# One common task order in each attention step becomes five, one for each engine, and a small tile moves

## The chip, the cores and the metric

One NeuronCore of one Trainium2 chip. The metric is the device time of one execution in microseconds, from the core's first to its last instruction with what lies around them. It has five engines with queues of their own: TensorE (PE), VectorE (DVE), ScalarE (ACT), GpSimd (POOL) and SyncE (SP), which here only issues DMAs.

## What is computed

Sixteen batches of 256 rows of 512 numbers (x) and of 256 rows of 384 (ctx) go through four residual blocks:

```python
x = x + _L0_xattn_ref(_layernorm(x), ctx_768, ctx_768, ...)   # q, k normed over the row; 16 heads of 32; + Qp, layer norm
x = x + _L0_ffn_ref(_layernorm(x), L0_ffn_weight)             # Hadamard turn, 4-bit rounding, ternary weight
x = x + _L1_xattn_ref(_layernorm(x), ctx_768, ...)            # 16 heads of 32, scores clipped at 1e4
x = x + _L1_ffn_ref(_layernorm(x), W1, b1, W2, b2)            # ternary 512 -> 2048, gelu, ternary 2048 -> 512
```

## The kernel before, in words

Products are made in float16 halves: a float32 operand is split into an upper half (a cast, on ACT) and a lower half (the rest, on DVE or POOL), and three products of halves stand for one. PSUM has 8 banks of 128x512 float32, and every product that is later read holds one.

The first three blocks run as a pipeline of four parts. Step i of 19 works on batch i in part "0f" (layer norm, query, key and value of attention 0), on batch i-1 in "0b" (the 16 heads of attention 0, its output, and the whole of the first feed-forward block), on batch i-2 in "1f" (the same front for attention 1, and the maxima of its scores), and on batch i-3 in "1b" (the heads of attention 1 and its output). Steps 3 to 15 have all four parts; I call them the steady steps. The last block is phase B, which comes behind the 19 steps and works on pairs of batches.

Each part is a list of tasks (`front_0`, `heads_of`, `back`, `front_1`). A task is a small piece that several engines share. What the lines of the profile are:

- `load` (SP, L657, L658, L663): fetches x and ctx of the next batch. For x it waits until the turned keys of the batch before have left the tile. `fetch` (SP, L643, L645, L650): the residual rows of a block; L650 is that of attention 1 and is needed by DVE at `out 1,0`.
- `stats` (DVE L1072, L1074, then POOL L783 to L789): mean and 1/deviation. `normalise` (ACT L887). `turn_x` (PE L1341 transposes, ACT L892 upper half, DVE L1083 lower half). `split_ctx` (ACT L910, DVE L1116).
- `project 0,k,j,late` (PE L1321 to L1325, each 128x512, 6 matmuls or 3): half of one projection. `bias` (ACT L917 squares or L925 upper half of a value, DVE L1126 or L1131). `unit` (ACT L932, DVE L1142). `unit_turn` (SP L688, DMA transposes).
- `project_turned` (PE L1331 to L1335), `split_qk` (ACT L943, DVE L1150).
- `scores` and `maxima` (PE L1473, 24 matmuls of 32 rows for four heads); `clip` (DVE L1169, attention 1 alone, in PSUM); `shift` (PE L1400, four matmuls that need all four clips); `reduce` (DVE L1157).
- `head l,n`: ACT takes exp of head n (L955) and the upper half of head n-1 (L963); POOL the lower half of head n-1 (L816); PE attends with head n-4 (L1495 to L1497, 12 matmuls of 33 or 32 columns, which wait for POOL's lower half); DVE divides four heads at a time (L1254). The exponentials lie in a ring of 5 slots (`pf`), the halves in rings of 4 (`ph`, `pl`): ACT's upper half of head h waits until PE has attended with head h-4.
- `out_project`, `out` (DVE L1185, L1188), `post_norm`, `turn_ffn`, `hadamard` (PE L1433), `absmax`, `round`, `levels`, `turn_levels` (SP L692), `ffn0` (PE L1443), `ffn0_out` (DVE L1223, POOL L828).
- In the last three steps `signs n` (DVE L1065 and L1067) makes the ternary weights of phase B, and `stats_b`, `norm_b` (L1077), `split_b` (L1089) and SP's transposes L611 its first input. PE's first matmuls of phase B are L1508.

The order is a string of digits: each takes the next task of that part's list. Every engine emits its instructions in this one order, skipping tasks in which it has nothing. The choice of banks (`banks_of`) is made from the same order. So an engine cannot be ahead of another in the order, only in time; it waits by semaphores.

```python
def task_order(i):
    ...
    order = ORDERS[i] if i in ORDERS else [n for n in ORDER if active[int(n)]]
    return [(PART[task], task) for task in merged(streams, order)]
...
def steps(emit):
    ...
        tasks = task_order(i)
        uses, counts = plan([task for _, task in tasks], base)
        emit(tasks, i, i % 2, {**kept, **uses})
```

## Time and profile before

| | us |
|---|---|
| median of 3 runs (lowest, highest) | 1842.26 (1839.59, 1843.07) |
| the profiled execution's own time | 1841.57 |
| its span, first to last instruction | 1839.7 |
| PE busy | 1651.1 (90%) |
| DVE busy | 1243.9 (68%) |
| ACT busy | 1017.6 (55%) |
| POOL busy | 987.0 (54%) |
| mean granted TensorE clock | 0.955 of full |

A share of busy time is a mean over stages. Matmuls are pipelined and their ends are modelled, so a stretch in which PE is "busy" can hold more or less work; PE's idle time and who ended it, and the chain of work followed back from the end, say more. The granted clock is 1.00 at 2.4 GHz and 0.50 at 1.2 GHz; in a row over a longer stretch it is the mean.

### The profile page before, as it was taken

What the parts mean: (1) busy time and instruction counts of PE and PEld (TensorE: products, weight loads), DVE (VectorE), ACT (ScalarE), POOL (GpSimd) and SP (SyncE); (2) the same over time, 40 slices, a digit from 0 to 9 for tenths busy, and PEclk for the clock granted to TensorE, in tenths of its full rate; (3) what the DMA queues carried; (4) which work ended last, traced back from release to release, by engine and by line L of the source; (5) the groups of instructions that cost most, each with busy time, mean ns of one, the idle gap of its engine ahead of it and who ended that gap; (6) DMA issues with size and microseconds to landing.
All of it is one profiled execution on the core that took longest, in us unless ns stands there. A gap on an engine that the chain in (4) does not pass through costs nothing.

```text
span 1839.7 us, 43874 instructions
## 1 busy us (share of the span) xinstructions
PE 1651.1 (90%) x17746; PEld 952.3 (52%) x17746; DVE 1243.9 (68%) x2428; ACT 1017.6 (55%) x1873; POOL 987.0 (54%) x1073
## 2 busy tenths in 40 slices
PE   5688999999999999989999999987748999999999
PEld 2445656556565555655556565564423444444444
DVE  4758778797887978779788787858873444343432
ACT  4663867658686585866758677586342222222221
POOL 2653857658585585856758576582461323322231
PEclk9889999999999999999999999978859999999999
DMA  7132231312304133131431313246222221221210
GB/s 249 53 112 58 68 113 25 113 40 87 113 14 114 30 107 97 29 113 28 110 93 34 113 28 111 63 138 195 92 73 54 69 69 32 60 61 54 69 47 23
DMA packets 168215, 144.80 MB, mean 79 GB/s; under 512 B 125256, under 2 KB 131528, under 8 KB 166992
## 3 DMA queue, kind: packets, MB, share of 16 engines
q1 hardware_dynamic: 165712, 133.62, 25.9%
q0 software_dynamic: 2304, 8.39, 1.1%
q8 instruction: 142, 2.33, 0.5%
q14 instruction: 57, 0.47, 0.1%
HBM read 72.77 MB, written 31.46 MB: 57 GB/s over the span
## 4 chain that ended last, share of the span: by engine, by line
PE 50%; DVE 27%; DMA 7%; issue 6%; ACT 5%; POOL 4%; SPq 1%; DVEq 1%; ACTq 0%; POOLq 0%
PE psum L1518 10%; PE psum L1508 9%; DVE psum L1169 6%; PE psum L1321 5%; PE psum L1322 5%; PE psum L1325 5%; DVE arena L1157 4%; PE psum L1473 4%; PE psum L1433 3%; PE psum L1341 2%; DMA arena<-in_x 2%; DVE arena L1072 2%; DVE arena L1198 2%; DMA out<-arena 2%; PE psum L1495 2%
## 5 line engine op out<-in xcount | busy, mean ns | idle before, releaser
L816 POOL TENSOR_TENSOR arena<-arena 128x512 f16<-128x512 f32 x512 | 597.8, 1190 | 125.9 <-ACT arena L963 125.9
L955 ACT ACTIVATE arena<-psum 128x512 f32<-128x512 f32 x512 | 304.9, 603 | 81.1 <-PE psum L1400 63.6
L963 ACT ACTIVATE arena<-arena 128x512 f16<-128x512 f32 x512 | 323.8, 640 | 16.5 <-PE psum L1497 16.5
L1321 PE MATMUL psum<-arena 128*128 128x512 f16 x672 | 263.9, 393 | 21.6 <-DVE arena L1083 15.1
L1006 ACT ACTIVATE arena<-psum,arena 128x512 f32<-128x512 f32 x128 | 88.0, 687 | 338.5 <-PE psum L1508 338.5
L1322 PE MATMUL psum<-arena 128*128 128x512 f16 x672 | 262.2, 390 | 0.0
L1325 PE MATMUL psum<-arena 128*128 128x512 f16 x672 | 261.6, 389 | 0.0
L848 POOL TENSOR_TENSOR arena<-arena 128x512 f16<-128x512 f32 x64 | 79.8, 1247 | 326.1 <-DVE arena L1276 326.1
L1508 PE MATMUL psum<-arena 128*128 128x512 f16 x1024 | 243.7, 381 | 8.0 <-DMA arena<-arena 8.0
L1518 PE MATMUL psum<-arena 128*128 128x512 f16 x1016 | 240.1, 379 | 3.3 <-POOL arena L848 3.2
L1495 PE MATMUL psum<-arena 128*128 128x33 f16 x2048 | 192.7, 180 | 44.8 <-POOL arena L816 43.4
L1276 DVE CAST arena<-arena 128x512 f16<-128x512 f32 x128 | 55.4, 433 | 253.0 <-ACT arena L1006 253.0
L1495 PEld LDWEIGHTS psum<-arena 128*128 128x128 f16 x2048 | 166.5, 97 | 90.5 <-issue 40.6
L828 POOL TENSOR_TENSOR arena<-arena 128x512 f32<-128x512 f32 x32 | 40.4, 1268 | 289.3 <-DVE arena L1223 288.5
L1473 PE MATMUL psum<-arena 32*128 32x256 f16 x4608 | 165.7, 276 | 29.7 <-ACT arena L955 7.9
L1497 PE MATMUL psum<-arena 128*128 128x33 f16 x2048 | 189.9, 178 | 0.0
L1496 PE MATMUL psum<-arena 128*128 128x32 f16 x2048 | 189.9, 178 | 0.0
L1169 DVE TENSOR_SCALAR psum<-psum 128x512 f32<-128x512 f32 x256 | 160.6, 690 | 42.6 <-PE psum L1473 42.5
L1496 PEld LDWEIGHTS psum<-arena 128*128 128x128 f16 x2048 | 164.3, 97 | 16.2 <-issue 1.0
L1508 PEld LDWEIGHTS psum<-arena 128*128 128x128 f16 x1024 | 100.6, 98 | 130.6 <-issue 11.2
L1518 PEld LDWEIGHTS psum<-arena 128*128 128x128 f16 x1016 | 98.8, 98 | 125.0 <-POOL arena L848 6.7
L1497 PEld LDWEIGHTS psum<-arena 128*128 128x128 f16 x2048 | 162.7, 97 | 0.0
(125 smaller groups left out, 3085.7 us busy)
## 6 DMA issues: line engine op xcount, KB each, us to landing
arena<-in_x SPq DMA_DIRECT2D x32, 512.0 KB, 4.3
arena<-x_scratch SPq DMA_DIRECT2D x32, 512.0 KB, 3.9
arena<-in_L_ffn_W SPq DMA_DIRECT2D x16, 1024.0 KB, 5.4
arena<-arena SPq DMA_DIRECT2D x16, 512.0 KB, 6.2
x_scratch<-arena POOLq DMA_DIRECT2D x16, 512.0 KB, 5.6
x_scratch<-arena SPq DMA_DIRECT2D x16, 512.0 KB, 3.0
out<-arena SPq DMA_DIRECT2D x14, 512.0 KB, 4.2
arena<-in_ctx SPq DMA_DIRECT2D x16, 384.0 KB, 5.3
```

The source lines that it names most:

```text
L816: gp.tensor_tensor(pl[l][:, h % NP, :], pf[l][:, h % NF, :], ph[l][:, h % NP, :], ALU.subtract).then_inc(p_lo[l].sem, 1)
L955: sc.activation(pf[l][:, h % NF, :], bank(u.bank), ACT.Exp, scale=SCALE / (QS * QS) if l == 0 else SCALE).then_inc(read[u.bank], 1)
L963: sc.activation(ph[l][:, h % NP, :], pf[l][:, h % NF, :], ACT.Copy).then_inc(p_hi[l].sem, 1)
L1169: v.tensor_scalar(bank(u.bank), bank(u.bank), CLAMP / SCALE, -CLAMP / SCALE, ALU.min, ALU.max).then_inc(clipped.sem, 1)
L1321: te.matmul(out, x_hi, w[:, 0, c, :], start=(c == 0), stop=False)
L1322: te.matmul(out, x_hi, w[:, 1, c, :], start=False, stop=False)
L1325: mm = te.matmul(out, x_lo, w[:, 0, c, :], start=False, stop=(c == chunks - 1))
L1495: te.matmul(out, p_hi_t, vs[l][:, k, h, 0:OW], start=(k == 0), stop=False)
L1496: te.matmul(out[:, 0:HD], p_hi_t, vs[l][:, k, h, HD + 2:VP], start=False, stop=False)
L1497: mm = te.matmul(out, p_lo_t, vs[l][:, k, h, 0:OW], start=False, stop=(k == NT - 1))
L1508: mm = te.matmul(bank(4 + f % 2), w1T[:, c, f * P:(f + 1) * P], xTb[slot][:, part, c, :], start=(c + part == 0), stop=(c + part == DC))
L1518: mm = te.matmul(bank(k), src[:, f % NG, k * P:(k + 1) * P], w2T[:, f, :], start=(f + n == 0), stop=(f + n == FC))
```

## The change

`task_order` and `steps` take an engine, and the tables hold one string for each of SP, POOL, ACT, DVE and PE in each step (one set, "steady", for steps 3 to 15). Banks and semaphore counts follow PE's order. Every task and every instruction is kept; only their order on each engine differs. The tile `row_of` (the rows that choose a bias) shrinks from 8 words to 2 and moves from the front of SBUF to a place just ahead of `vs`. All tiles between start 8 words lower; `vs`, `levels0` and the rings `pf` and `ph` start 6 words lower, so at 8 bytes past a multiple of 64 where they were at 32. Two targets of DMA transposes in the rings (`nT` and `xTb`) begin 6 words further in and so keep their addresses.

```diff
-ORDER = ("2001111112202000110100120110101030111011033113331200330301313312003311031123031121332233310133333313"
...
 ORDERS = {
...
+    "steady": {
+        "SP": ("2010000000000000000011111111111111111111111111111111111111111111111111100000000031333333333333333333"
...
+ENGINES = ("SP", "POOL", "ACT", "DVE", "PE")
...
-def task_order(i):
+def task_order(i, engine):
...
-    order = ORDERS[i] if i in ORDERS else [n for n in ORDER if active[int(n)]]
+    order = ORDERS.get(i, ORDERS["steady"])[engine]
...
-def steps(emit):
+def steps(emit, engine):
...
-        tasks = task_order(i)
-        uses, counts = plan([task for _, task in tasks], base)
-        emit(tasks, i, i % 2, {**kept, **uses})
+        uses, counts = plan([task for _, task in task_order(i, "PE")], base)
+        emit(task_order(i, engine), i, i % 2, {**kept, **uses})
...
-        row_of = take(8)[:, 0:2].bitcast(F16)
...
+        row_of = take(2).bitcast(F16)
...
-        nT = ph_raw[0][:, NT * D // 2:NT * D].bitcast(F16).rearrange("p (c n) -> p c n", c=DC)
+        nT = ph_raw[0][:, NT * D // 2 + 6:NT * D + 6].bitcast(F16).rearrange("p (c n) -> p c n", c=DC)
...
-        xTb = [pf_raw[0][:, 0:DC * BT * P].bitcast(F16).rearrange("p (s c n) -> p s c n", s=2, c=DC)]
+        xTb = [pf_raw[0][:, 6:DC * BT * P + 6].bitcast(F16).rearrange("p (s c n) -> p s c n", s=2, c=DC)]
```

In the changed kernel every line of the engines' bodies stands 68 lower (L955 is L1023 there).

First place: PE in a steady step, around the `shift` of the first four heads of attention 1. Before, behind the attention matmuls of head 12:

```order
L1497 MATMUL psum<-arena 128x33
L1400 MATMUL psum<-arena 128x512 x4
L1321 MATMUL psum<-arena 128x512
L1322 MATMUL psum<-arena 128x512
L1325 MATMUL psum<-arena 128x512
```

Now, behind those of head 13:

```order
L1565 MATMUL psum<-arena 128x33
L1389 MATMUL psum<-arena 128x512
L1390 MATMUL psum<-arena 128x512
L1393 MATMUL psum<-arena 128x512
L1389 MATMUL psum<-arena 128x512
L1390 MATMUL psum<-arena 128x512
L1393 MATMUL psum<-arena 128x512
L1468 MATMUL psum<-arena 128x512 x4
L1563 MATMUL psum<-arena 128x33
```

The shift has moved behind one more head (13) and behind half a projection. Also, the two halves of `project 0,1,0`, which stood on either side of the attention of head 5 (task `head 0,9`), now stand on either side of that of head 9 (task `head 0,13`).

Second place: ACT in a steady step, the two squares of the query (L917, now L985) among the heads of attention 0. Before:

```order
L963 ACTIVATE arena<-arena 128x512
L917 ACTIVATE arena<-arena 128x512
L955 ACTIVATE arena<-psum 128x512
L963 ACTIVATE arena<-arena 128x512
L955 ACTIVATE arena<-psum 128x512
L963 ACTIVATE arena<-arena 128x512
L917 ACTIVATE arena<-arena 128x512
L955 ACTIVATE arena<-psum 128x512
```

Now:

```order
L1031 ACTIVATE arena<-arena 128x512
L985 ACTIVATE arena<-arena 128x512
L1023 ACTIVATE arena<-psum 128x512
L1031 ACTIVATE arena<-arena 128x512
L985 ACTIVATE arena<-arena 128x512
L1023 ACTIVATE arena<-psum 128x512
```

The first square stood behind `head 0,9` and the second behind `head 0,11`; now they stand behind `head 0,13` and `head 0,14`, so the heads 9 to 12 no longer queue behind them.

Third place: DVE in the last of the 19 steps, around its last two `signs`. Before:

```order
L1067 SCALAR_TENSOR_TENSOR arena<-arena 128x2048
L1169 TENSOR_SCALAR psum<-psum 128x512 x4
L1251 RECIPROCAL arena<-psum 128x8
L1254 TENSOR_TENSOR arena<-psum,arena 128x128 x2
L1169 TENSOR_SCALAR psum<-psum 128x512 x4
L1251 RECIPROCAL arena<-psum 128x8
L1254 TENSOR_TENSOR arena<-psum,arena 128x128 x2
L1065 TENSOR_SCALAR arena<-arena 128x2048
L1067 SCALAR_TENSOR_TENSOR arena<-arena 128x2048
L1072 BN_STATS arena<-arena 128x6
```

Now:

```order
L1135 SCALAR_TENSOR_TENSOR arena<-arena 128x2048
L1237 TENSOR_SCALAR psum<-psum 128x512 x4
L1319 RECIPROCAL arena<-psum 128x8
L1322 TENSOR_TENSOR arena<-psum,arena 128x128 x2
L1133 TENSOR_SCALAR arena<-arena 128x2048
L1135 SCALAR_TENSOR_TENSOR arena<-arena 128x2048
L1237 TENSOR_SCALAR psum<-psum 128x512 x4
L1319 RECIPROCAL arena<-psum 128x8
```

The last `signs` has moved ahead of the last four clips.

SP in a steady step: `fetch 1` (the residual rows of attention 1, L650, now L718) stood ahead of the transposes, right behind the context's store. Now:

```order
L763 DMA ctx_scratch<-arena 128x768
L756 DMA_TRANSPOSE arena<-arena 128x8x128 x2
L760 DMA_TRANSPOSE arena<-arena 128x4x128
L756 DMA_TRANSPOSE arena<-arena 128x8x128 x2
L718 DMA arena<-x_scratch 128x1024
L760 DMA_TRANSPOSE arena<-arena 128x4x128
```

It now stands behind both `unit_turn`s and the first `turn_levels`, each of which waits for DVE.

## Rows read from the trace of the kernel before

**Rows 1.** Busy time by stretch: span, PE, PEld, DVE, ACT, POOL, granted clock, DMA, GB/s.

```profile
290.00:367.90 77.90, 72.89 (x978) 45.50 (x977) 61.78 (x127) 54.44 (x106) 51.73 (x59) 0.98 0.26 75
...
1068.40:1146.20 77.80, 72.77 (x979) 45.61 (x978) 61.60 (x128) 54.63 (x106) 51.63 (x59) 0.98 0.26 75
...
1300.00:1380.00 80.00, 47.69 (x641) 29.27 (x638) 61.82 (x96) 28.59 (x55) 39.71 (x28) 0.73 0.23 73
```

**Rows 2.** Chain of waits, 600 to 760: start, us, what (x's load in two steps).

```profile
643.90 5.12 DMA arena<-in_x
...
721.79 5.12 DMA arena<-in_x
```

**Rows 3.** Chain of waits, 640 to 680, around that load.

```profile
642.29 0.70 DVE arena L1185
...
654.77 1.84 DVE arena L1116
...
657.27 0.39 PE psum L1321
```

**Rows 4.** Busy time by stretch, as rows 1: heads of attention 0, and after.

```profile
648.30:671.00 22.70, 19.46 (x329) 13.79 (x328) 12.29 (x27) 22.12 (x44) 19.48 (x21) 0.99 0.36 130
664.50:670.60 6.10, 4.46 (x132) 3.39 (x127) 4.46 (x13) 5.82 (x13) 5.24 (x6) 0.99 0.01 3
670.60:674.00 3.40, 3.40 (x13) 1.24 (x10) 3.25 (x7) 3.40 (x7) 3.37 (x4) 0.52 0.02 5
```

**Rows 5.** Who PE waited for, 664.5 to 671: total us, times, longest.

```profile
PE psum L1495 <- POOL arena L816: 1.1, 2, 0.7
```

**Rows 6.** ACT in order of time: start, us, line, operation, [idle before <-releaser].

```profile
662.12 0.62 ACT L917 ACTIVATE arena<-arena 128x512 bf16<-128x512 f32 x1
...
664.78 0.63 ACT L963 ACTIVATE arena<-arena 128x512 f16<-128x512 f32 x1 [0.45 <-PE psum L1497]
```

**Rows 7.** POOL in order of time, lower halves of three heads.

```profile
669.99 3.38 POOL L816 TENSOR_TENSOR arena<-arena 128x512 f16<-128x512 f32 x3
```

**Rows 8.** Chain of waits, 640 to 680: one matmul at either clock, four scores.

```profile
657.66 0.22 PE psum L1322
...
659.03 0.77 PE psum L1473 x24
...
671.22 0.43 PE psum L1322
```

**Rows 9.** DVE in order of time: `unit` beside an idle POOL, then a busy one.

```profile
628.33 1.47 DVE L1142 SCALAR_TENSOR_TENSOR arena<-arena 128x512 f16<-128x512 f32 x2
...
672.34 2.25 DVE L1142 SCALAR_TENSOR_TENSOR arena<-arena 128x512 f16<-128x512 f32 x2
```

**Rows 10.** DVE in order of time: a residual add, `out 1,0`.

```profile
640.31 0.69 DVE L1185 SCALAR_TENSOR_TENSOR arena<-psum,arena 128x512 f32<-128x512 f32 x1
```

**Rows 11.** DMAs that touch the scratch tensors, whole program.

```profile
DMA to landing us min/median/max: 2.7/3.9/7.7
```

**Rows 12.** DVE in order of time, last step.

```profile
1355.77 2.49 DVE L1169 TENSOR_SCALAR psum<-psum 128x512 f32<-128x512 f32 x4 [4.49 <-PE psum L1473]
...
1358.81 1.28 DVE L1065 TENSOR_SCALAR arena<-arena 128x2048 f16<-128x2048 f32 x1
1360.12 3.34 DVE L1067 SCALAR_TENSOR_TENSOR arena<-arena 128x2048 f16<-128x2048 f32 x1
```

**Rows 13.** Chain of waits, 1340 to 1400.

```profile
1360.15 7.66 POOL arena L816 x5
...
1379.88 0.61 DVE arena L1089
...
1386.60 3.59 PE psum L1508 x8
```

**Rows 14.** ACT in order of time: a write into the values' tile, one elsewhere.

```profile
645.97 0.60 ACT L925 ACTIVATE arena<-psum 128x512 f16<-128x512 f32 x1 [6.97 <-PE psum L1325]
...
651.74 0.61 ACT L943 ACTIVATE arena<-psum 128x512 f16<-128x512 f32 x1
```

103 lines of the change are left out of this document (84 added, 19 removed).

## The prediction

> **What bounds the kernel now.** I read the busy time by stretch first. From 290 to 1146 us it shows 11 equal stretches of which the first and the last stand in [rows 1]; PE is busy some 73 of 77.8 us in each and DVE 62. So PE is the bound, with little slack, and whatever the change saves in a step it saves 13 times. The chain of waits gives the step's length, as the distance of two equal events: 721.79 - 643.90 = 77.89 us [rows 2]. The third row of [rows 1] is part of the drain, the last steps before phase B, where PE is busy 47.7 of 80 us at a mean clock of 0.73: most idle time for each step lies there.
>
> PE's idle time in a steady step is one thing and its wasted time another. I cut the step along the chain into pieces:
>
> Piece A, the load. The residual add `out 1,1` ends (642.29 + 0.70), only then does SP issue x's load, which lands 5.12 us after 643.90; statistics, normalising, transposes and `split_ctx` follow, and PE's first projection starts at 657.27 [rows 2, 3]. The chain is 14.3 us long, and PE fills most of it with other work.
>
> Piece B, the heads of attention 0, 648.3 to 671.0. ACT is busy 22.1 of 22.7 us and PE only 19.5 [rows 4]: here ACT, not PE, is full. In its last part PE waits 1.1 us for POOL's halves [rows 5], and ACT once waits 0.45 for PE to release a ring slot [rows 6]. So the ring goes round through all three.
>
> Piece C, right behind. From 670.60 the granted clock is 0.52, that is the 1.2 GHz level, for 3.4 us; in the 6.1 us before, at 2.4 GHz, PE was busy 4.5 us, all of it attention matmuls of 33 columns and 32-row scores [rows 4]. In 9 of the 11 stretches the mean is 0.98 as in [rows 1], in two it is 1.00: the fall comes in most steps. It hits projections: 0.43 us a matmul where 0.22 is usual [rows 8]. Eight of them lose 1.7 us.
>
> The Trainium skill ("TensorE: Matmul & The Clock Gate", Part 1) says that idleness throttles the array and sustained activity releases it. By that alone this fall would not be there, since no wait of PE near it is over 0.7 us, and the change could not take it away. The trace disagrees: the clock falls behind a stretch that is 73% busy.
>
> **The change part by part, steady steps.** All counts are per step.
>
> 1. ACT's two squares go behind heads 13 and 14 instead of 9 and 11. Each costs 0.62 us [rows 6], so heads 10 and 11 come 0.6 us sooner on ACT and head 12 1.2 us sooner, and PE's attention, which has 2 halves of a projection less ahead of it, releases the slots before ACT asks (the 0.45 goes). What is late next is POOL: 3.38 / 3 = 1.13 us a head [rows 7], which cannot start before 652.4, when it has made the deviations. 14 heads end at 652.4 + 14 x 1.13 = 668.2. I walk PE beside that: the projection starts at about 658.3 (ACT now does one more head before the context's split, but it starts 0.5 sooner; DVE does `split_qk 1,1,1`, 0.6 us, ahead of the first `split_x`), so 1.0 later than 657.27, but with one more head and a `scores` task done, 1.2 us of work (0.77 and the wait at its start [rows 8]; a head is 12 matmuls 25 ns apart, 0.3). PE then finds every head ready until head 13 and starts the next projection at 668.8; before, it started at 670.6, a head (0.3) less and a shift (0.4) more done. Gain 1.8 + 0.3 - 0.4 = 1.7 us.
> 2. The clock. The narrow stretch shrinks from 6.1 us to the 2.6 us between the second half of `project 0,1,0` and the next projection. I expect the fall to go there. It is worth 1.7 us on PE.
> 3. DVE takes this back in part. `stats 1` (1.7 us) is out of its way, but behind the scores of 667.1 it has four clips, the guard, a division, `unit` (2.25 beside a busy POOL [rows 9]), a division, two clips, a bias and two clips: the second shift can go at 676.8 to 677.1, before at 679.2. So of 1.7 + 1.7 = 3.4 us, 2.1 to 2.4 are kept. DVE is late next.
> 4. `split_out` and `turn_x 1,1`: PE waits some 0.3 us more for DVE there. Kept: 1.8 to 2.0.
> 5. `unit 0,1` moves ahead of `split_ffn 0,1`, from beside an idle POOL (1.47 us for two) to beside a busy one (2.25) [rows 9]. It delays the second Hadamard by 0.2 us; what follows waits for the values' biases, which come when they did. The `unit` itself is off the path. Cost 0 to 0.2. If one sorts by the Trainium skill instead ("SBUF — State Buffer", Who interferes with whom: a DVE instruction with two SBUF inputs and a GpSimd one that reads SBUF exclude each other), each of the two would stand a whole POOL subtraction; the row shows 0.4 more for each, so I keep the row.
> 6. The tail of the step: `shifts 1,1` moves ahead of the last bias and of `ffn0_out`, and the next step's scores start 0.5 us sooner; but `out 1,1` has one more `reduce` before it, and the load chain starts 0.2 later. As piece A is set by the load, not by PE, the 0.5 buys nothing and the 0.2 is paid.
> 7. SP's `fetch 1` is issued behind the transposes, at about 633.5. It lands 3.9 us later [rows 11], so at 637.4 to 638, and is wanted at about 639 (640.31 before [rows 10], the queue ahead of it shorter). Cost 0 now; the cover is one microsecond.
>
> Sum for a steady step: -1.8 us, times 13: **-23.4 us**.
>
> **The last step.** DVE idles 4.49 us before its last clips, and behind them spends 1.28 + 3.34 on the last `signs` [rows 12]. Now the `signs` fill the idle time. POOL's last five halves, on the chain, took 7.66 us beside them [rows 13], 5 x 1.13 = 5.65 without: 2.0 us. Then `norm_b` and `split_b` no longer queue behind the residual adds: the last `split_b` ended at 1380.5 and gated the transposes and PE's first matmul at 1386.60 [rows 13]; it needs four norms (0.5), two output splits (0.7), four splits (0.6 to 1.2) behind the last division, about 8.3 us from 1366.7 instead of 11.6 from 1368.9. **-5.5 us**.
>
> **The other five ragged steps** (0, 1, 2, 16, 17). Every order differs. No row prices that. From below: an order made for each engine could cost as much as it saves, +3. From above: PE waits about 70 us there, most for chains through DVE that no order shortens; a quarter is 17. I take **-4**, nearer the low end since the tasks at the longest waits (the `turn_ffn` of step 1, the shifts of step 17) keep their places.
>
> **The tile.** The rings now start 8 bytes past a multiple of 64. The nearest rows are ACT's cast into the values' tile, whose rows lie 132 bytes apart, 0.60 us, and the same cast into an even tile, 0.61 [rows 14]. So 0. A price is kept among the rivals.
>
> Sum: -23.4 - 5.5 - 4 = -33 us on the profiled execution's own 1841.6 us; its median is 0.7 higher. **Forecast 1809 us.**
>
> **The rivals.**
> - The clock falls all the same, in piece C or before the first projection, where heads 0 to 3, two transposes and a `scores` now stand together, 5 us of narrow work. For it: that stretch is nearly as long as today's. Against: a wide `project_turned` stands right ahead of it, and today's front, 4 us long, brings no fall. Half a projection before the shift and half behind it, at half clock, put the next scores 1.9 us later, of which DVE hides 0.7: 1.2 us a step. 13 x 0.6 + 9.5 = 17: **1825 us**.
> - The gain does not go round. Piece A runs from DVE's `out 1,1` to the load and is not shortened by the change. If PE's denser pieces only make it wait longer for the load (DVE, 62 of 78 us, leaves the end of the step no room), only the last step's 5.5 stays: **1836 us**.
> - Slower: the late residual. DVE's `out 1,0` stands in line ahead of `out 1,1`, and that issues x's load. If `fetch 1` lands later than 1 us behind my reckoning, each step is longer by the rest. The landing times go up to 7.7 us [rows 11]: then 7.7 - 3.9 - 1.0 = 2.8 us x 13 = 36, **1845 us**. It decides from a landing of 7.4 us on. Against: 3.9 is the median, and six small transposes are its only company.
> - The rings' place costs. Every head's work on POOL, ACT and PE touches them. In piece B POOL is late next, so 0.3 us on each subtraction is 16 x 0.3 = 4.8 us a step, x 13 = 62: **1871 us**. It decides from 0.16 us on each (1.13 to 1.29).
> - The orders could hold only in name, if a semaphore made an engine wait for what the common order implied. None is added, and the waits name the task that they need. Under 1 in 100.
>
> **How the numbers follow.** A measurement of this kernel can tell a change from no change from about 0.2% (3.7 us) on. Forecast 0.55, clock 0.2, no round 0.11, late residual 0.08, rings 0.06. The range goes down to 1797, for up to 12 us more from the ragged steps or 0.9 more a step, and up to 1836, so that the two slower rivals and half of the tail of the third are left out. Faster: 0.55 + 0.2 + 0.11 less a part that ends within 3.7 us, 0.84; within 0.2%: 0.06; slower: 0.10.
>
> **What would show it.** The distance of two x loads is 76.1 us. The granted clock reads 1.00 in most stretches of a step. PE's wait for POOL in piece B is under 0.6 us. POOL's subtraction stays 1.13 us from start to start. `out 1,0` waits for PE and not for a DMA. In the last step DVE's `signs` lie before the last clips and phase B's first matmul starts 5 to 6 us earlier, counted from the last `shift`. Wrong if the step stays over 77.3, if the last of PE's waits is for DVE's L1237, or if the clock still reads 0.98.

## The result, and the profile after

The changed kernel takes **1827.84 us** (median of 4 runs, 1825.35 to 1830.4) against 1842.66 for the kernel before (4 runs beside them): ratio 0.9923, 95% interval 0.9904 to 0.9943. It is faster, by 14.8 us where 33 were forecast. Its profiled execution took 1826.25 us, with a span of 1823.8 (1839.7 before).

Every line of the changed kernel stands 68 lower than before: POOL's subtraction L816 is L884, the shift L1400 is L1468, `unit` L1142 is L1210, the residual add L1185 is L1253.

Busy time by stretch of the kernel after. The first row is one step from load to load, beside [rows 1]; the next two are the two longest steps; the last two are a piece of attention 0's heads and what follows it, beside [rows 4].

```profile
800.73:877.04 76.31, 72.08 (x981) 45.29 (x979) 62.70 (x128) 54.56 (x105) 50.71 (x58) 1.00 0.28 76
500.40:578.40 78.00, 73.59 (x986) 45.69 (x982) 62.62 (x127) 54.86 (x107) 50.87 (x59) 0.98 0.24 69
578.40:658.40 80.00, 73.88 (x997) 46.62 (x994) 62.59 (x127) 54.82 (x107) 52.21 (x60) 0.98 0.27 79
...
821.40:827.50 6.10, 5.96 (x110) 3.49 (x109) 4.01 (x11) 5.82 (x14) 5.61 (x7) 1.00 0.01 3
827.50:830.90 3.40, 3.32 (x56) 1.95 (x53) 3.37 (x7) 3.40 (x8) 3.16 (x6) 1.00 0.63 43
```

The piece in which PE was 73% busy is now 98% busy, and the clock behind it reads 1.00 in place of 0.52. The chain of waits, x's load in two steps, and below it the same for the longest step:

```profile
800.73 5.04 DMA arena<-in_x
...
807.94 0.21 POOL arena L852
808.21 0.73 POOL arena L853
809.20 4.92 POOL arena L884 x4
...
877.04 5.55 DMA arena<-in_x
```

```profile
569.36 4.09 DMA arena<-in_x
...
644.52 7.40 DMA arena<-in_x
```

This step is 877.04 - 800.73 = 76.31 us against 77.89 in [rows 2]; the ten steps without a fall of the clock (I call them quiet) take 75.16 to 77.51, 76.55 in the mean. Most of that spread is the load's: from its landing to PE's first shift there are 21.2 us in each quiet step, and so there were before. Two steps are not quiet: in that from 500.4 the clock fell, and in that from 578.4 it fell and the load took 7.40 us to land.

The page's groups of POOL's subtraction and of its add, before and after (total us, mean ns):

```profile
L816 POOL TENSOR_TENSOR arena<-arena 128x512 f16<-128x512 f32 x512 | 597.8, 1190 | 125.9 <-ACT arena L963 125.9
...
L828 POOL TENSOR_TENSOR arena<-arena 128x512 f32<-128x512 f32 x32 | 40.4, 1268 | 289.3 <-DVE arena L1223 288.5
```

```profile
L884 POOL TENSOR_TENSOR arena<-arena 128x512 f16<-128x512 f32 x512 | 579.8, 1160 | 116.6 <-ACT arena L1031 114.8
...
L896 POOL TENSOR_TENSOR arena<-arena 128x512 f32<-128x512 f32 x32 | 34.4, 1094 | 302.1 <-DVE arena L1291 302.1
```

The same two instructions are shorter, and I had forecast that they would not be. In order of time POOL did 13 subtractions in 14.48 us, 1.11 each where [rows 7] had 1.13 by the same division; one of the 13 took 1.80, and those that nothing disturbs start 1.05 apart, for 1.11 to 1.12 before:

```profile
809.16 14.48 POOL L884 TENSOR_TENSOR arena<-arena 128x512 f16<-128x512 f32 x13
```

PE's waits in that step, and DVE around the two Hadamard products of attention 0 in it:

```profile
PE psum L1563 <- POOL arena L884: 2.2, 4, 1.1
PE psum L1501 <- DVE arena L1151: 0.6, 1, 0.6
```

```profile
853.91 0.68 DVE L1151 TENSOR_TENSOR arena<-psum,arena 128x512 f16<-128x512 f32 x1
854.51 3.16 DVE L1210 SCALAR_TENSOR_TENSOR arena<-arena 128x512 f16<-128x512 f32 x2
857.59 0.68 DVE L1151 TENSOR_TENSOR arena<-psum,arena 128x512 f16<-128x512 f32 x1
```

`unit 0,1` (L1210) stands between the two splits (L1151) that the products wait for, and took 3.16 us where I had priced 2.25 [rows 9]. Taken one by one, beside POOL, the two of [rows 9] and, below them, the two here:

```profile
672.22 1.15 POOL L816 TENSOR_TENSOR arena<-arena 128x512 f16<-128x512 f32 x1
...
672.34 1.58 DVE L1142 SCALAR_TENSOR_TENSOR arena<-arena 128x512 f16<-128x512 f32 x1
...
673.84 0.74 DVE L1142 SCALAR_TENSOR_TENSOR arena<-arena 128x512 f16<-128x512 f32 x1
```

```profile
854.51 1.66 DVE L1210 SCALAR_TENSOR_TENSOR arena<-arena 128x512 f16<-128x512 f32 x1
854.53 1.09 POOL L884 TENSOR_TENSOR arena<-arena 128x512 f16<-128x512 f32 x1 [1.22 <-ACT arena L1031]
...
855.58 1.54 POOL L884 TENSOR_TENSOR arena<-arena 128x512 f16<-128x512 f32 x1
...
856.09 1.57 DVE L1210 SCALAR_TENSOR_TENSOR arena<-arena 128x512 f16<-128x512 f32 x1
```

So 2.25 was no price for two beside a busy POOL: the first met a subtraction and took 1.58, the second met none and took 0.74. The first ended 0.55 us after the subtraction that it met (672.22 + 1.15 = 673.37, 672.34 + 1.58 = 673.92), and so did both of the later two (0.55 after 855.62 and 0.54 after 857.12). The subtraction that starts beside a waiting `unit` is longer too, 1.54 for 1.09.

The last step, chain of waits, beside [rows 12, 13]:

```profile
1350.63 0.61 PE psum L1468 x4
...
1363.56 3.34 DVE arena L1157 x2
...
1369.59 3.17 DMA arena<-arena
...
1372.90 1.90 PE psum L1576 x8
```

From the last shift to phase B's first matmul there are 1372.90 - 1350.63 = 22.3 us; before, 1386.60 - 1358.32 = 28.3 with the matmul of [rows 13] and this row for the shift:

```profile
1358.32 0.61 PE psum L1400 x3
```

**Where the time went.** I cut both traces at `split_ctx` of step 3 and of step 15 and at phase B's first matmul. Steps 0 to 2: 187.7 us before, 192.7 after, **+5.0**. Twelve steady steps: 933.0 and 925.2, **-7.8**. The drain from there: 265.9 and 254.9, **-11.0**. Phase B, whose order is untouched: 453.1 and 450.9, -2.2. Together -15.9, the difference of the spans.

### The profile page after: what moved, and what is told of

Read it like the earlier page. It is cut to its first block, busy times and chain, and to the rows that moved or that the text cites. A ratio compares the mean times of both kernels' runs of the same rounds, so it can differ in the third digit from the quotient of the medians.

```text
span 1823.8 us, 43897 instructions
## 1 busy us (share of the span) xinstructions
PE 1638.3 (90%) x17746; PEld 945.1 (52%) x17746; DVE 1242.2 (68%) x2428; ACT 1015.8 (56%) x1873; POOL 959.1 (53%) x1073
## 4 chain that ended last, share of the span: by engine, by line
PE 46%; DVE 31%; POOL 8%; DMA 6%; issue 4%; ACT 2%; SPq 2%; DVEq 1%; ACTq 0%; POOLq 0%
PE psum L1586 11%; PE psum L1576 11%; DVE psum L1237 8%; POOL arena L884 6%; PE psum L1389 4%; PE psum L1393 4%; PE psum L1390 4%; DMA arena<-in_x 4%; PE psum L1541 3%; DVE arena L1225 3%; DVE arena L1140 3%; DVE arena L1210 3%; DVE arena L1322 2%; DVE arena L1266 2%; DVE arena L1151 2%
## 5 line engine op out<-in xcount | busy, mean ns | idle before, releaser
L884 POOL TENSOR_TENSOR arena<-arena 128x512 f16<-128x512 f32 x512 | 579.8, 1160 | 116.6 <-ACT arena L1031 114.8
L1023 ACT ACTIVATE arena<-psum 128x512 f32<-128x512 f32 x512 | 307.0, 606 | 89.0 <-PE psum L1468 66.7
L1389 PE MATMUL psum<-arena 128*128 128x512 f16 x672 | 259.8, 387 | 12.3 <-DVE arena L1091 8.5
L1390 PE MATMUL psum<-arena 128*128 128x512 f16 x672 | 258.7, 385 | 0.0
L1393 PE MATMUL psum<-arena 128*128 128x512 f16 x672 | 258.1, 384 | 0.0
L1563 PE MATMUL psum<-arena 128*128 128x33 f16 x2048 | 194.8, 180 | 64.4 <-POOL arena L884 58.8
L916 POOL TENSOR_TENSOR arena<-arena 128x512 f16<-128x512 f32 x64 | 79.8, 1248 | 322.4 <-DVE arena L1344 322.4
L1576 PE MATMUL psum<-arena 128*128 128x512 f16 x1024 | 241.7, 379 | 1.9 <-DMA arena<-arena 1.9
L1586 PE MATMUL psum<-arena 128*128 128x512 f16 x1016 | 240.1, 379 | 3.2 <-POOL arena L916 3.2
L896 POOL TENSOR_TENSOR arena<-arena 128x512 f32<-128x512 f32 x32 | 34.4, 1094 | 302.1 <-DVE arena L1291 302.1
L1565 PE MATMUL psum<-arena 128*128 128x33 f16 x2048 | 191.8, 178 | 0.0
L1564 PE MATMUL psum<-arena 128*128 128x32 f16 x2048 | 191.8, 178 | 0.0
```

The lines of the kernel that those rows point to most:

```text
L884: gp.tensor_tensor(pl[l][:, h % NP, :], pf[l][:, h % NF, :], ph[l][:, h % NP, :], ALU.subtract).then_inc(p_lo[l].sem, 1)
L1023: sc.activation(pf[l][:, h % NF, :], bank(u.bank), ACT.Exp, scale=SCALE / (QS * QS) if l == 0 else SCALE).then_inc(read[u.bank], 1)
L1389: te.matmul(out, x_hi, w[:, 0, c, :], start=(c == 0), stop=False)
L1390: te.matmul(out, x_hi, w[:, 1, c, :], start=False, stop=False)
L1393: mm = te.matmul(out, x_lo, w[:, 0, c, :], start=False, stop=(c == chunks - 1))
L1563: te.matmul(out, p_hi_t, vs[l][:, k, h, 0:OW], start=(k == 0), stop=False)
```

## The experiments

Each kernel is given by its median and by its ratio, with the 95% interval, to the kernel before on the same chip; 0.001 of the ratio is 1.84 us. Lines stand lower in the variants than in the changed kernel; each is named where it is used. A fall is one of TensorE's clock from 2.4 to 1.2 GHz, counted in the twelve steps from step 3 to step 15.

**1. The small tile alone** (`tile_only`): the kernel before with

```diff
-        row_of = take(8)[:, 0:2].bitcast(F16)
...
         unit_rows = xn0.bitcast(F16).rearrange("p t (s n) -> p t s n", s=2)
+        row_of = take(2).bitcast(F16)
...
-        nT = ph_raw[0][:, NT * D // 2:NT * D].bitcast(F16).rearrange("p (c n) -> p c n", c=DC)
+        nT = ph_raw[0][:, NT * D // 2 + 6:NT * D + 6].bitcast(F16).rearrange("p (c n) -> p c n", c=DC)
...
```

> The kernel before with its common order, and only the tile moved (rings and levels0 at 8 bytes past a multiple of 64). In the changed kernel POOL's subtraction lasts 1.09 us where it lasted 1.16, and the sum of the levels 1.09 where it was 1.27. Theory 1, the place of the tiles does it: here too 1.09 and 1.09, and 1 to 6 us less in all, since POOL ends PE's waits in the heads of attention 0. Rival, the new order keeps VectorE out of POOL's way: 1.16 and 1.27 stay, and the time is that of the kernel before, 1842.

**2. The orders alone** (`orders_only`): the changed kernel with the tile put back in the same way.

> The changed kernel with the tile back in its old place. Theory 1 (place): the subtraction is back at 1.16 us, and as POOL makes the first heads that PE waits for in each step, 4 to 14 x 0.06 us a step are lost, 3 to 10 us in all: 1831 to 1838. Rival (order): 1.09 stays, time as the changed kernel, 1828. If the orders alone bring nothing it is 1842.

Measured: the tile alone 1833.74 us, 0.9959 (0.9945 to 0.9973), -7.6 us; the orders alone 1836.62 us, 0.9971 (0.9961 to 0.998), -5.3 us. The profiled execution of the tile alone was the slowest of its six, 1838.81. The page's groups of the run with the tile alone, and of the one with the orders alone:

```profile
L816 POOL TENSOR_TENSOR arena<-arena 128x512 f16<-128x512 f32 x512 | 563.1, 1121 | 155.8 <-ACT arena L963 155.1
...
L848 POOL TENSOR_TENSOR arena<-arena 128x512 f16<-128x512 f32 x64 | 79.8, 1246 | 325.6 <-DVE arena L1276 325.6
...
L828 POOL TENSOR_TENSOR arena<-arena 128x512 f32<-128x512 f32 x32 | 34.9, 1093 | 295.0 <-DVE arena L1223 294.9
```

```profile
L884 POOL TENSOR_TENSOR arena<-arena 128x512 f16<-128x512 f32 x512 | 614.8, 1229 | 100.2 <-ACT arena L1031 99.7
...
L916 POOL TENSOR_TENSOR arena<-arena 128x512 f16<-128x512 f32 x64 | 79.8, 1247 | 322.6 <-DVE arena L1344 322.6
...
L896 POOL TENSOR_TENSOR arena<-arena 128x512 f32<-128x512 f32 x32 | 39.9, 1267 | 299.2 <-DVE arena L1291 299.2
```

So the tile's place, and nothing of the orders, makes the subtraction 69 ns shorter (1190 to 1121, 1229 to 1160) and the add 175 ns. The orders make the mean 39 ns longer again, and the traces show how: with the old orders 10 and 12 of the 512 subtractions take over 1.4 us, with the new ones 52 and 54, of which 26 stand beside `unit` and 12 or 13 beside DVE's `split_ctx`; the medians are 1158 ns in the old place and 1090 in the new with either order. A third instruction of POOL (L848, in phase B, 1246) reads as in the run with the orders alone, 1247.

**3. Steps 0 to 2 back** (`old_start`): the changed kernel, where `COMMON` holds the strings of before.

```diff
+for n in (0, 1, 2):
+    ORDERS[n] = dict.fromkeys(ORDERS[n], COMMON[n])
```

> The changed kernel, with steps 0, 1 and 2 in the common order of before on every engine. Step 3's first split of a context began at 187.7 us before and at 192.7 in the changed kernel. Theory: the new orders of the first steps lose these 5 us, so 187 to 189 and 1823 in all. Rival: the start is late by its first loads and the clock, which differ from run to run: 190 to 193 and 1828.

Measured: 1815.1 us, 0.9862 (0.9849 to 0.9875), 11 to 13 us faster than the full change. Step 3 begins at 186.8 us in place of 192.7, and the twelve steady steps take 917.1 in place of 925.2. The theory had 1823 us: the start costs more than what lies ahead of step 3. It costs about as much as the new steady orders bring (10.5 us, experiment 9).

**4. Steps 16 to 18 back** (`old_end`): the same for `B`, `B + 1`, `B + 2`.

> The changed kernel, with steps 16, 17 and 18 in the common order of before. From step 15's split of the context to the end it took 719.0 us before and 705.8 in the changed kernel. Theory: the new orders of the end bring this, 13 us, so 1840 to 1842 in all and a first matmul of phase B 13 us later. Rival: half of it is POOL's faster subtraction and the clock, then 1833 to 1836.

Measured: 1830.0 us, 0.9938 (0.9926 to 0.9951). The intervals of this and of the change overlap; in the profiled runs the drain took 262.4 us in place of 254.9, so these orders bring 7.5 us there, of which the median shows 2 to 3. Both expectations (1840 to 1842, 1833 to 1836) missed. From the last shift to phase B there are 28.6 us again, as with the tile alone (28.6), so the 6 us gained there are the orders' and not the tile's.

**5. and 6. Which of the first steps** (`old_step0` with `for n in (0,)`, `old_steps12` with `for n in (1, 2)`).

> The changed kernel, with step 0 alone back on the one order of before (the small tile, steps 1 and 2, the steady steps and the end stay changed). The run with steps 0 to 2 back took 1815.1 us against 1827.8 for the change. Theory A, step 0 is what costs (its new orders put weight splits of ACT and DVE behind the first normalise and split_ctx work, and TensorE waits 12.5 us for ACT in the first 50 us): 1814 to 1819 us, and the twelve steady steps as in that run, 917 to 920 us. Rival B, steps 1 and 2 cost (they leave the steady steps a worse phase between transfers and chains): 1824 to 1829 us. Rival C, both share it: 1819 to 1824 us.

> The complement: steps 1 and 2 back on the order of before, step 0 stays changed. Theory A (step 0 costs): 1824 to 1829 us, step 3 begins at 190 to 194 us as after the change. Rival B (steps 1 and 2 cost): 1814 to 1819 us, step 3 begins at 187 us. Rival C (both): in between. If the parts don't add, with both runs at 1815 or both at 1828, it is the pairing of one order with the next that counts.

Measured: 1820.47 us, 0.9877 (0.9862 to 0.9893), step 3 at 187.8 us; and 1823.42 us, 0.9888 (0.9871 to 0.9906), step 3 at 190.7. Each put back brings 8.5 and 6.4 us by the ratios, and all three steps together 11.2 (the intervals leave room for a plain sum). Ahead of step 3 lie 5 to 6 of these: it begins at 191.8 to 194.3 us in the three profiled executions with all the new orders of the start, at 183.8 to 192.0 (mean 187.5) in the thirteen with all the old ones. The rest lies in steady steps whose orders are the same, 8 us in the two profiled runs (925.2 and 917.1). Of the 8, some 4 are falls and one slow load: in the change one step had a load of 7.40 us and a fall, another a fall; with steps 0 to 2 back one of twelve had a fall and no load took over 5.7. The other 4 are in the quiet steps, 76.7 for 76.36 us in the mean, cut at `split_ctx`. The times of the change (1825.35 to 1830.4) and of this run (1813.85 to 1819.15) don't overlap, so most of it comes with the kernel; why the beginning decides what happens in the steady steps was not shown.

**7. and 8. Step 0, by engine** (`s0_act`: `ORDERS[0]["ACT"] = COMMON[0]`; `s0_actdve`: ACT's and DVE's).

> The changed kernel with ACT's order of step 0 alone back on that of before; DVE, TensorE, POOL and the transfers keep their new orders there. Theory: what step 0 loses is on ACT, where the new order puts normalise, split_ctx and the first x split ahead of the third and fourth weight split (TensorE's first 12.5 us wait is for ACT's split of x): step 3 begins at 188 us, as with the whole of step 0 back, and 1820 to 1823 us. Rival: it is on DVE, whose weight splits stand behind the context's: step 3 at 191 to 193 us, 1826 to 1829 us.

> The changed kernel with the orders of ACT and DVE of step 0 back on that of before; with ACT's alone step 3 began at 194.2 us, no earlier than after the change. Theory, what step 0 loses at the start is on DVE's weight splits: step 3 begins at 187 to 189 us as with all five orders back, and 1818 to 1822 us. Rival, it is TensorE's or POOL's order: step 3 at 192 to 195 us and 1823 to 1828 us.

Measured: 1823.46 us, 0.9893 (0.9875 to 0.9911), with step 3 at 194.2 us; and 1822.94 us, 0.989 (0.9874 to 0.9906), with step 3 at 187.8. ACT's order alone gives the start nothing; ACT's and DVE's together give it all of the 4.9 us, by one profiled execution each. The medians are the same within the interval. In the profiled executions the second is 6.5 us shorter, as its start says (the twelve steady steps take 921.6 and 921.5), but that execution was the fastest of its four (1817.72 of 1817.72 to 1826.56); where the others give the gain back was not shown. DVE in order of time in the kernel after (a weight's split is L1091), and below it with both orders back (L1105):

```profile
13.87 0.96 DVE L1184 TENSOR_TENSOR arena<-arena 128x768 f16<-128x768 f32 x1 [5.36 <-ACT arena L978]
...
37.65 2.29 DVE L1091 SCALAR_TENSOR_TENSOR arena<-arena 128x2048 f16<-128x2048 f32 x1 [2.81 <-ACT arena L936]
```

```profile
11.62 4.09 DVE L1105 SCALAR_TENSOR_TENSOR arena<-arena 128x1536 f16<-128x1536 f32 x2 [3.13 <-ACT arena L950]
...
30.31 2.29 DVE L1105 SCALAR_TENSOR_TENSOR arena<-arena 128x2048 f16<-128x2048 f32 x1
```

DVE stands 5.36 us for the context's upper half with weights behind it, and the last weight's split begins 7.3 us later.

**9. What the steady orders are worth** (`os_old_steady`): as 3, and `"steady"` back too; left are the tile and the end's orders.

> Steps 0 to 2 and the steady steps back on the order of before: what is left of the change is the moved small tile and the new orders of steps 16 to 18. Theory: the steady orders are worth what the twelve steps show between the run of the tile alone (924.4 us) and the run with steps 0 to 2 back (917.1 us), 7.3 us in twelve and 8 in thirteen steps, so 1815.1 + 8 = 1823 us, with 7 to 9 falls of the clock in the twelve steps. Rival: the steady orders carry the 23 us that I forecast for them less the tile's 7.5, some 16 us: 1831 us. Second rival: the gain of 1815.1 was the common start alone, and the steady orders give nothing: 1815 to 1817 us.

Measured: 1828.25 us, 0.9919 (0.9905 to 0.9933), so the steady orders bring 0.0057, 10.5 us, with the tile moved, between the theory's 8 and the rival's 16. Nine of the twelve steps have a fall, as before the change; they take 77.8 us in the mean, the other three 76.8. With the new orders (3) eleven steps have none and take 76.36.

**10. The tile's place under the new orders** (`os_tileback`): as 3, with the tile put back.

> The run of 1815.1 us (steps 0 to 2 in the order of before, all else as changed) with the small tile back at its first place, so that the subtraction takes 1.158 us again in place of 1.090. Theory, the tile's place is worth in the new orders what it was worth alone or between the two versions (7.5 us alone, 8.8 us between orders alone and the full change): 1822 to 1825 us, quiet steps 77.0 us against 76.35. Rival, with the new orders TensorE waits less for POOL and the place matters little: 1815 to 1819 us. Second rival: it also decides how often the clock falls: over 1826 us.

Measured: 1832.67 us, 0.9938 (0.9926 to 0.9951) against 0.9862: the tile is worth 14 us here, almost twice its 7.6 alone, and the time is in the range of the second rival, by which the place also decides how often the clock falls. A quiet step gains no more than under the old orders: 0.7 us, from 77.07 to 76.36, as from 77.12 to 76.45 with the tile alone. The rest of this run's 13 us in twelve steps is three steps with a fall (78.8) for one. PE waits for POOL's subtraction 3.3 us in a step with the orders alone, 2.2 to 2.4 with the tile moved, 1.1 before. Whether the place causes the falls or they vary from run to run was not tested.

**11. The thin stretch made long again** (`os_narrow`): as 3, and both halves of `project 0,1,0` on PE alone put forward, behind `project 0,0,0,1` and `head 0,10`.

> Steps 0 to 2 on the order of before, as in the run of 1815.1 us, and in the steady steps two projections of TensorE (both halves of chunk 1 of tile 0) put forward again, out of the stretch of heads, so that this stretch has matmuls of heads alone, as before the change; the residual shift keeps its new place. Theory, the thin stretch is what lets the clock fall: 7 to 12 falls in the twelve steps against 1, at about 1 us each, 1822 to 1828 us. Rival, the falls went for another reason (the transposes of the next step, the transfers): 0 to 2 falls, and 1814 to 1818 us. Second rival: the projections in their old place make the heads wait less for POOL and the step is shorter: under 1813 us.

Measured: 1894.26 us, 1.028 (1.0261 to 1.0299). The clock fell 14 times, at least once in each of the twelve steps, and the shortest took 82.1 us. That is 5.8 over a quiet step of 3, where steps with a fall are 0.8 to 2.6 us longer in the other runs, so the falls are not likely to be all of it. No theory of mine gave this number. The shift keeps its new place in this run, and nine of the 14 falls begin within 3.1 us ahead of it.

**12. A wide piece put into the thin stretch** (`fill`): as 9, and

```diff
+later("steady", "PE", (("project", 0, 1, 0, 1), ("head", 0, 13)))
```

> The run with the small tile moved, new orders in steps 16 to 18 alone and everything else in the order of before (1828.3 us, nine falls of the clock in twelve steady steps), with one edit: in the steady steps TensorE does the second half of chunk 1 of tile 0's projection after head 0,13 in place of before head 0,10, so that wide matmuls stand in the thin stretch of heads. No other engine's order is touched. Theory, the thin stretch is what lets the clock fall, and a fall costs a step 0.8 to 1.0 us there (steps with a fall 77.8 us in the mean, without 76.8): 0 to 3 falls, twelve steps 924 to 926 us against 930.3, and 1821 to 1824 us in all. Rival, a stretch of heads isn't enough and the falls need the new places of ACT and DVE as well: 7 to 9 falls and 1826 to 1830 us. Second rival: the falls go, but the later projection is late for its bias and costs as much: 0 to 3 falls, 1828 us or more.

Measured: 1884.26 us, 1.0231 (1.0216 to 1.0246), 12 falls, a step 81.7 us. ACT in that step:

```profile
605.10 0.70 ACT L1062 ACTIVATE arena<-arena 128x512 f16<-128x512 f32 x1
608.55 0.63 ACT L1016 ACTIVATE arena<-arena 128x512 bf16<-128x512 f32 x1 [2.75 <-DVE arena L1225]
```

The squares (L1016) of the piece that was put off stand in ACT's row ahead of the next head's exp; ACT idles 2.75 us, and PE waits 3.1 for ACT in that step. One engine's move without the others' costs 4.2 us a step, four times what a fall costs in 9. As the banks of PSUM follow PE's order, a move on PE also changes their choice, here and in 11, 14 and 15; that was not separated.

**13. The same with its partners** (`fill_three`): also

```diff
+later("steady", "ACT", (("bias", 0, 1, 0), ("head", 0, 14)))
+later("steady", "DVE", (("bias", 0, 1, 0), ("head", 0, 12)))
```

> As the run that moved the second half of chunk 1's projection behind head 0,13 on TensorE alone and took 1884.3 us, but now ACT's bias 0,1,0 (the squares of that chunk) moves with it, behind its head 0,14, and DVE's bias 0,1,0 behind its head 0,12; all else is the order of before with the small tile moved (1828.3 us without the moves, 81.7 us a step against 77.6 with TensorE's alone). In that run ACT stood 2.75 us at the squares with the heads' scaling behind them. Theory A, the 56 us were that one queue on ACT, and a thin stretch with a wide piece in it keeps the clock: 0 to 3 falls in the twelve steps, 1819 to 1824 us. Rival B, the queue on ACT is mended but the falls come from elsewhere: 7 to 12 falls and 1826 to 1832 us. Rival C, the piece is late for what follows it whatever ACT does (norm, unit, the next clips on DVE): over 1850 us, as before.

Measured: 1844.73 us, 1.0005 (0.9996 to 1.0014), 11 falls, a step 78.8 us. ACT's queue was some 40 of the 56 us; the falls are still there, as rival B had it, but the time is 13 us over that rival's.

**14. and 15. The whole piece of the new order** (`stretch`: TensorE's three late halves behind heads 0,10, 0,12 and 0,13, ACT's two bias tasks behind 0,13 and 0,14, DVE's two behind 0,12; `stretch_shift`: the same and `("shift", 1, 0), ("head", 0, 17)` on PE).

> Orders of before in steps 0 to 15 with the small tile moved (1828.3 us, nine falls), and in the steady steps the whole piece of the new order between head 0,8 and head 0,14 put in, on three engines at once: TensorE's three late halves of projections behind heads 0,10, 0,12 and 0,13, ACT's two bias tasks behind its heads 0,13 and 0,14, DVE's two behind its head 0,12. The run that moved one of these halves with its bias (1844.7 us, eleven falls) left the stretch ahead of it thinner. Theory A, it is this piece that keeps the clock up: 0 to 3 falls in the twelve steps and 1817 to 1823 us. Rival B, the piece only fits with the rest of the new order (x's turns and the split of attention 1's queries ahead of it): 7 to 12 falls, 1835 to 1850 us, a step of 78 us or more.

> The same, with one move more on TensorE: shift 1,0 behind head 0,17, so that from head 0,8 on its whole stretch stands nearly as in the new order. Theory A: the shift is the last piece, and where the run without it has falls this one has 0 to 3, 1817 to 1822 us. Rival B: same falls and time as the run without it, within 2 us; then the place of the falls stays open and I say so.

Measured: 1861.98 us, 1.0119 (1.0102 to 1.0135), with 14 falls; and 1840.3 us, 1.0002 (0.9993 to 1.0012), with 2. The busy time around the place, in a step without the shift's move and in one with it:

```profile
675.10:683.60 8.50, 6.92 (x133) 4.35 (x131) 3.88 (x10) 6.64 (x15) 5.39 (x6) 0.90 0.01 2
683.60:690.40 6.80, 5.93 (x53) 2.82 (x57) 4.85 (x12) 5.82 (x11) 5.68 (x9) 0.50 0.28 55
```

```profile
666.50:675.00 8.50, 8.31 (x147) 4.74 (x136) 5.07 (x14) 7.76 (x17) 6.85 (x8) 1.00 0.01 2
675.00:681.80 6.80, 4.67 (x66) 3.08 (x62) 6.62 (x15) 6.13 (x13) 5.68 (x8) 1.00 0.41 80
```

PE's wait at this shift, in a step of `stretch` and, below it, in one of run 9, where all of the old steady order stands:

```profile
PE psum L1501 <- DVE psum L1270: 2.5, 1, 2.5
```

```profile
PE psum L1483 <- DVE psum L1252: 0.4, 1, 0.4
```

In `stretch` one move of four matmuls takes the falls from 14 to 2. Where PE stood at the shift, which waits for DVE's four clips, with the projection behind it, it was busy 6.9 of 8.5 us and the clock fell (its 0.90 is the end of an earlier fall); with both halves of the projection first it is busy 8.3 of 8.5. It is worth 22 us here. But that wait was 2.5 us, where the order of before has 0.4 and falls all the same: putting the wide pieces late had taken away the work that PE did while DVE clipped. And the shift's new place alone does not keep the clock up, since run 11 has it and 14 falls. Of what was run, only both together, late wide pieces and a late shift, leave 1 to 3 falls; the late shift with the old places of all else was not run. Without falls the step is still 78.05 us, since the rest of the orders does not fit; the new orders as a whole reach 76.36.

**16. `unit 0,1` put back** (`os_unit`): as 3, and

```diff
+moved("steady", "DVE", (("unit", 0, 1), ("absmax", 0, 1)))
```

> The run with steps 0 to 2 in the order of before (1815.1 us), and in the steady steps DVE's unit 0,1 back behind absmax 0,1, as before the change, nothing else. Theory: those two instructions (2.50 us) stand on the chain of waits ahead of the split for hadamard 0,0 and 0,1, where TensorE waits 0.6 us, so each step gains 0.3 to 0.6 us: 1808 to 1812 us. Rival: the transposes of the unit rows and the load of x behind them on SP come later by as much (the load waits for those transposes): 1815 to 1820 us. Second rival: the clock is disturbed where TensorE's wait was: over 1820 us.

Measured: 1812.49 us, 0.984 (0.9823 to 0.9857). The interval overlaps that of 3 (0.9849 to 0.9875); in the traces the way from the first Hadamard product to `out 1,1` is 0.37 us shorter in each step (19.96 and 20.33), but the load lands later and the quiet step as a whole is 76.31 for 76.36. It shows in the whole step once the load is out of the way (18).

**17. x's load 9 us earlier** (`early_x`): as 3, and

```diff
                     if kind == "load":
-                        load_front(l, b, use)
+                        if l == 1 or i - 1 in ORDERS or i == B:
+                            load_front(l, b, use)
...
                         fetch(l, b)
+                        if l == 1 and i not in ORDERS and i + 1 < B:
+                            load_front(0, i + 1, use)
```

> The run with steps 0 to 2 in the order of before (1815.1 us), and in the steady steps the transfer of the next batch's x and context is put in SP's row behind fetch 1, some 9 us earlier, in place of behind the store of attention 1's result, whose last instruction on DVE gates it (863.47 us, the load 865.15 us in a step). Nothing is left out. Theory, the step is a loop through this load: DVE would begin the statistics when it is done with the feed-forward output (868.9 us in place of 870.5), POOL its own when it has issued the store (871.4 in place of 872.4), and every step is 1.0 to 1.6 us shorter: 1796 to 1804 us. Rival, the loop has a second member of almost the same length (TensorE is busy for 71.7 of 76.3 us): 0 to 0.4 us a step, 1810 to 1815 us. Second rival: the earlier transfer takes the 16 DMA engines from the transposes and the context's fetch, TensorE waits for these, or the clock falls again: 1815 us or more.

Measured: 1813.13 us, 0.9841 (0.9828 to 0.9854). SP's queue: x's load (L740) no longer waits for the store (L799).

```profile
854.55 0.38 SPq L740 DMA_DIRECT2D arena<-in_x  x1
...
862.65 0.38 SPq L799 DMA_DIRECT2D x_scratch<-arena  x1
```

A quiet step takes 75.9 us (75.8 to 76.1, nine of them) in place of 76.36, the first rival; the other three have a fall (77.3), for one in 3, and the spread that the landing made is gone. PE's waits in one step of run 3, and below it of this one: the wait for POOL went from 2.4 us to 1.2, and one of 1.1 for ACT came.

```profile
PE psum L1578 <- POOL arena L899: 2.4, 4, 1.1
```

```profile
PE psum L1581 <- POOL arena L902: 1.2, 4, 0.4
PE psum L1559 <- ACT arena L1041: 1.1, 1, 1.1
```

The load was in the loop, with 0.4 us of lead over the next member in a quiet step.

**18. Both** (`early_unit`).

> Both edits on the run of 1815.1 us that each gained something alone: DVE's unit 0,1 behind absmax 0,1 (1812.5 us) and x's transfer behind fetch 1 (1813.1 us). Theory, they act at two places of the loop and add: 75.6 us a quiet step, 1809 to 1811 us. Rival, both only shift the same wait: 1812 to 1814 us. Second rival: the unit rows' transposes come later and the transfer of x behind them with them, so the second edit's gain is lost: 1813 to 1816 us.

Measured: **1808.27 us**, 0.9805 (0.9792 to 0.9818), the fastest kernel of this study; each edit alone had brought 0.0021 to 0.0022 from 0.9862, so they add; the 2 us more than the sum are within the intervals. Quiet steps take 75.5 to 75.8, 75.55 in the mean for 75.92 in 17: here `unit`'s 0.37 us is in the whole step. It beats the changed kernel by 1.2%.

## Why the prediction was wrong

The forecast was -33 us: -23.4 for thirteen steady steps, -5.5 for the last, -4 for the other five, 0 for the tile. The traces and runs put in its place: the steady orders 0.25 us a step without the tile and 0.8 with it (10.5 us in thirteen), the tile -14 under the new orders (its share of falls, start and phase B in it), the first three steps +11 with what they do later, the drain -11. These overlap and are not a sum. The term that failed most is the steady step: 1.8 us were forecast for each of thirteen, and the orders alone gave 0.25.

The steady step, cut at x's load, the first matmuls of three shifts, the first Hadamard product and the start of `out 1,1`, means in us over steps:

| from, to | before, 9 steps with a fall | before, 3 without | new orders, tile back, 9 quiet | changed, 10 quiet |
|---|---|---|---|---|
| load, shift 1,0 | 26.3 | 26.1 | 26.6 | 26.3 |
| shift 1,0, shift 1,1 | 8.9 | 8.3 | 6.1 | 6.0 |
| shift 1,1, shift 1,3 | 19.7 | 19.8 | 20.1 | 20.0 |
| shift 1,3, Hadamard 0,0 | 1.9 | 1.9 | 1.9 | 1.9 |
| Hadamard, `out 1,1` | 19.3 | 19.3 | 20.5 | 20.3 |
| `out 1,1`, next load | 1.6 | 1.9 | 1.9 | 2.0 |
| in all | 77.8 | 77.3 | 77.05 | 76.55 |

**Items 1 to 3 came out.** I had the second shift 2.1 to 2.4 us earlier; it is 8.9 - 6.1 less 0.3 for a later first one, 2.5 us. The clock's falls went from 9 to 2 in twelve steps. My reason, that the stretch of heads without wide work lets the clock fall, is neither refuted nor enough. Wide pieces put into it with the shift left in place (12 to 14) left 11 to 14 falls, but they also made PE's wait at the shift longer, 0.4 us to 1.3 and 2.5; the shift's place without the wide pieces (11) left 14; both (15, and the change) leave 2. What a fall costs I had as 1.7 us on PE, of which DVE takes most back; by the lengths of steps, cut at `split_ctx`, it is 0.8 (77.96 and 77.13 before), so that part stands. In a step of the change it is more: with the fall 3.7 us behind `split_ctx` the first shift comes 22.7 us after the load's landing, for 21.2.

**Items 4 to 6 are the step that failed.** I took 0.3 off for item 4, 0 to 0.2 for `unit 0,1` and 0.2 for the tail. The table has +0.4, +1.2 and +0.3, against the kernel before with a fall: 1.9 us given back, so that of 2.5 only 0.7 are left, and against the steps without a fall 0.2. On `unit` the error has a name. I priced its instructions (2.25 us for 1.47) and took it for off the path, but it stands in DVE's row between the two splits that the two Hadamard products wait for: 3.16 us at 854.51, and the second product starts 3.5 us behind the first where it was 2.0. Put back behind `absmax` (16) it returns 0.37 us of that stretch. Most of what is left is the one more `reduce` that item 6 had named and priced at 0.2. The reduces alone (L1157, now L1225) between the first Hadamard product and `out 1,1`, before and after: the span, DVE's busy time in them and their number, clock, DMA share, GB/s:

```profile
623.01:642.29 19.28, 6.93 (x11) 1.00 0.22 42
```

```profile
854.85:875.17 20.32, 7.44 (x12) 1.00 0.28 60
```

They take 0.5 us more, in a stretch where DVE is idle for 1.3 us of 20.3. With the tile moved the stretch is 1.04 longer than before: 0.37 for `unit`, and 0.67 of which that is most. That DVE had no room at the end of the step I had written myself, in the rival by which the gain does not go round; what I put in front of `out 1,1` there is paid nearly in full.

I also read [rows 9] wrongly. The 0.4 us more for each was the mean of one instruction that met a subtraction (0.84 more than 0.74) and one that met none. With the new order both meet one: 1.58 us each (3.16 / 2), 0.85 over the 0.73 of one that is left alone. In the steady steps each `unit` that takes over 0.9 us ends 0.54 or 0.55 us after a subtraction of POOL's does; 33 of 44 do so where 11 of 45 did. The Trainium skill ("SBUF — State Buffer", Who interferes with whom) says that a DVE instruction with two inputs in SBUF and a GpSimd one that reads SBUF lock each other out. The trace agrees: `unit` ends only 0.55 us after the subtraction that it met, and the next subtraction takes 1.54 us for 1.09. As a price I had read it as a whole subtraction on each, 1.05 to 1.10 us; what is left of the one that is running, 0.85, is what was paid.

**The tile was a mis-sized term.** Nearest rows were ACT's casts into an odd and an even tile, 0.60 and 0.61 us [rows 14]; I read from one engine what another would do. POOL's subtraction became 69 ns shorter in the mean. Of the rival with the opposite sign the mechanism was right (the place sets POOL's time, and POOL is late next), only it went down. Its working gives 0.069 x 16 = 1.1 us a step, 14 in thirteen steps, and 14 was measured, but that is luck: a quiet step gained 0.7, and falls and the start made up the rest (10).

**The first steps failed in sign.** I took -4 for all five ragged steps and gave +3 as their worst. The three at the start cost 11 us (3), of which 5 lie ahead of step 3, for DVE's and ACT's weight splits (8). Steps 16 and 17 gained about 1 us (7.5 in the drain less 6.3 behind the last shift, 4). That no row priced them I had said; that the term could reach 11 I had not. Their effect on steady steps I had no term for at all.

**The last step was right.** -5.5 forecast, 28.3 - 22.3 = -6.0 measured, by the mechanism named: the last `signs` lie ahead of the last clips, and with the end's old orders the 28 us are back (4).

**The rivals.** "The clock falls all the same" named the place before the first projection. The two falls that are left in the change lie elsewhere than before: one 3.7 us behind `split_ctx`, which is that place, and one near the end of a step. It was right about the place: over the twelve profiled kernels with the new steady orders (run 11 aside), 24 of 25 falls begin 0.6 to 4.7 us behind `split_ctx`. It happened in 1 to 3 of twelve steps and cost more than my 1.2 us: cut at `split_ctx`, steps with a fall take 78.0 and, with a slow load, 80.0 in place of 76.7. "The gain does not go round" was half right: the load is in the loop (21.2 us from its landing to the first shift in every quiet step), and most of the steady gain did not go round; but moved 9 us forward it gave only 0.4 us a step (17), so the next member is hardly shorter. Its 1836 us is what the orders alone took (1836.62), by other sums. "Late residual" did not happen; the profile shows no idle time ahead of `out 1,0` in a steady step.

**By the signs named.** The load distance is 76.55 in the mean of the quiet steps (76.1 forecast); the clock reads 1.00 in most; phase B starts 6.0 us sooner. Three failed: POOL's subtraction did not stay at 1.13, PE's wait for POOL went up, 2.2 us in the step shown for 1.1 in a step before, and `out 1,0` waits for neither PE nor a DMA, since DVE is never idle ahead of it.

## What to carry to other kernels

When a pipeline's step is a loop through several engines, walk the whole loop and not the half where the change pays: what is moved out of one piece stands in a row somewhere else, and its price is its place between two things that are waited for, not its duration. Orders of several engines are one design: a single task moved on PE alone cost 4.2 us a step, most of it through ACT's queue, more than all the orders together had gained. A row with two instructions in it is no price for one: look at each, and at what it met on the other engine. Test the parts of a large change one by one; here 11 us lay in undoing its first three steps, and with two small edits more 0.9923 became 0.9805.

## What the hardware showed unexpectedly

A GpSimd subtraction of the same shape took 1121 ns in place of 1190 in the mean, and an add 1093 in place of 1268, when the tiles they touch were moved by a few bytes; a third, in phase B, read 1246 and 1247. Which of the tiles' starts decides was not tried. A DVE instruction that met a GpSimd subtraction took 1.57 to 1.66 us in place of 0.74 and ended 0.55 us after it, and the next subtraction took 1.54 for 1.09. TensorE's clock fell 14 times in twelve steps where four matmuls that wait 2.5 us for DVE stood ahead of a projection, and 2 times where they stood behind it; but in another order they stood behind half of it and it fell 14 times too. And a load of 512 KB, 5.3 us in the median, took 7.40 once in the profiled execution, in a kernel whose transfers had only moved by some microseconds.
